# A four-layer modulated convolution and a mixture of experts on one core: layer 3 run one group later, routing two, tap matrices placed by the host, the first inputs scaled first

## The reference

```python
# x: (128 samples, 32 channels, 512 positions); four convolution layers, K = 3,
# whose weights are modulated per sample by a style and then normalised
s = style @ mw.T + mb
weight = SCALE * w * s[:, None, :, None]
demod = lax.rsqrt(jnp.sum(weight * weight, axis=(2, 3)) + EPS)
# layer 0 'same'; layer 1 'upsample' (transposed, stride 2, then blur);
# layer 2 'same'; layer 3 'downsample' (blur, then stride 2)
# its result, read as 4096 tokens of 512, goes through 16 experts, the best 4 for each token
scores = jax.nn.sigmoid(x @ gate_w.T) + bias
topk_w, topk_idx = jax.lax.top_k(scores, TOPK)
z = jax.nn.silu(x @ Wg.T) * (x @ Wu.T)            # for each expert, 256 wide
out = sum_over_chosen(weight * (z @ Wd.T)) + shared_expert(x)
return x_input + out
```

## Time and profile before

| | |
|---|---|
| three runs | 1251.31, 1252.97 (median), 1257.61 us |
| profiled execution | 1261.94 us, span 1260.2 us |
| PE busy, share of the span | 91% |
| DVE / ACT / POOL busy | 63% / 39% / 46% |
| mean clock granted to PE | 0.969 of full speed |
| first phase, to the last `place` | 569 us |

### The profile page before, as it was taken

How to read it: one execution, slowest core, us unless ns; L and a number is a source line. 1 busy time by engine, 2 the same in 40 slices (tenths; PEclk the granted TensorE clock), 3 DMA queues, 4 the chain that set the end, 5 groups by cost and what they waited for, 6 DMA issues and landing times. The chain is left out here.

```text
span 1260.2 us, 24634 instructions
## 1 busy us (share of the span) xinstructions
PE 1147.9 (91%) x7160; PEld 1001.8 (79%) x7161; DVE 799.0 (63%) x1979; ACT 497.6 (39%) x1164; POOL 577.8 (46%) x667
## 2 busy tenths in 40 slices
PE   3799998989898988772999999999999999999995
PEld 2577777777777766662999999999998889999995
DVE  6667776767776767655665565655656665555653
ACT  4555555555554545330332232323324332222321
POOL 1001423232323233344566656666566566666663
PEclk9999999999999999975999999999999999999998
DMA  4565444444444534314667676676766777666664
GB/s 147 134 178 140 135 133 134 134 130 137 132 135 117 146 108 132 90 34 118 150 119 157 115 157 118 124 150 110 156 118 151 197 118 165 109 111 112 113 113 74
DMA packets 141625, 162.42 MB, mean 129 GB/s; under 512 B 33120, under 2 KB 98720, under 8 KB 140064
## 3 DMA queue, kind: packets, MB, share of 16 engines
q0 software_dynamic: 35696, 74.34, 33.1%
q1 hardware_dynamic: 104608, 87.78, 23.9%
q10 hardware_dynamic: 1296, 0.01, 0.1%
HBM read 73.41 MB, written 55.18 MB: 102 GB/s over the span
## 5 line engine op out<-in xcount | busy, mean ns | idle before, releaser
L1262 PE MATMUL bank<-xt_hi,wup_hi 128*128 128x256 f32 x1104 | 276.2, 283 | 1.7 <-ACT xt_hi L635 1.6
L1262 PE MATMUL bank<-xt_hi,wup_lo 128*128 128x256 f32 x1104 | 275.7, 282 | 0.0
L462 POOL DMA_INDIRECT out_rows<-yb,sid x140 | 227.4, 1625 | 91.2 <-DVE yb L1029 67.1
L1262 PEld LDWEIGHTS bank<-xt_hi,wup_hi 128*128 128x128 f32 x1104 | 209.9, 190 | 6.6 <-ACT xt_hi L635 2.0
L404 POOL DMA_INDIRECT lists<-entry,place x128 | 130.8, 1022 | 177.8 <-DVE place L854 100.9
L1262 PEld LDWEIGHTS bank<-xt_hi,wup_lo 128*128 128x128 f32 x1104 | 209.3, 190 | 2.7
L545 ACT ACTIVATE t<-bank,cB,cA 128x256 f32<-128x256 f32 (+1 forms) x384 | 172.2, 539 | 68.7 <-PE bank L217 66.4
L449 POOL DMA_INDIRECT xg<-h_rows,gid x140 | 142.2, 1015 | 122.5 <-PE bank L1240 80.8
L1266 PE MATMUL bank<-xt_lo,wup_hi 128*128 128x256 f32 x1104 | 176.5, 282 | 0.0
L1266 PEld LDWEIGHTS bank<-xt_lo,wup_hi 128*128 128x128 f32 x1104 | 151.4, 190 | 0.0
L1029 DVE TENSOR_SCALAR yb<-bank,all_lists 128x512 f32<-128x512 f32 x138 | 99.6, 748 | 79.9 <-DMA out_rows<-yb,sid 46.0
(11 more groups left out here) (212 smaller groups left out, 2169.5 us busy)
## 6 DMA issues: line engine op xcount, KB each, us to landing
x<-x1p SPq DMA_DIRECT2D x64, 384.0 KB
wraw<-in_Wup SPq DMA_DIRECT2D x11, 1024.0 KB
xraw<-in_xq SPq DMA_DIRECT2D x32, 260.0 KB
xbase<-in_x SPq DMA_DIRECT2D x32, 256.0 KB
h_rows<-hrow SPq DMA_DIRECT2D x128, 64.0 KB
out_rows<-orow SPq DMA_DIRECT2D x32, 256.0 KB
x<-x1p SPq DMA_DIRECT2D x64, 127.0 KB
wdraw<-in_Wdn SPq DMA_DIRECT2D x11, 512.0 KB
```

The source lines that it names most:

```text
L462: pool.indirect_dma_start(out=out, out_offset=bass.IndirectOffsetOnAxis(ap=sid[:, u:u + 1], axis=0), in_=yb[:, u, :], in_offset=None, comp ...
L1262: pe.matmul(dst, lhs[a], rhs[0], start=k == 0 and a == 0, stop=False)
```

## The change

Three things. The tap matrices come placed (and the sum of squares is taken on 32 partitions), so that only the blur's mix and the split remain on the chip; POOL scales two groups before it does anything else, and DVE's constants for the routing move behind the scales. The pipeline becomes deeper: body g runs layer 3 of group g - 1 and the stage of group g - 2, each one body later, and G + 3 bodies are run in place of G + 2. The banks are dealt out anew (layers 1 and 2 share banks 1 and 2, layer 3 has bank 3, the logits bank 4), and the steps within a body stand in another order on each engine.

```diff
+        MATRICES = ((placed, 0, FIRST, 2), (placed, 2, SAME, 2), (mixed, 0, UP, 1), (mixed, 1, DOWN, 3))
...
+        def bodies(eng, body, end):
+            for g in range(R + 1):
+                body(g, None, None)
+            with eng.Fori(0, ROUNDS - 1) as it:
+                for u in range(R):
+                    body(it * R + (R + 1 + u), it, u)
+            for g in range(LAST + 1, end):
+                body(g, None, None)
...
@@ SP
-            for q in range(Q):
-                sp.dma_start(wnat[C * q:C * q + C].rearrange("o l i k -> o l (i k)"),
             sp.dma_start(xraw[:, 0], xq[0]).then_inc(S["x_loaded0"], 16)
+            sp.dma_start(placed[:, PLACED_UP:PLACED_DOWN], placed_taps[:, PLACED_UP:PLACED_DOWN]).then_inc(S["placed_loaded1"], 16)
+            sp.dma_start(placed[:, PLACED_DOWN:], placed_taps[:, PLACED_DOWN:]).then_inc(S["placed_loaded2"], 16)
...
+            def body(g, it, u):
...
+                if within(g, 0, G - 3):
+                    sp.wait_ge(S["x0_hi"], g + 2)
...
+                if within(g, 3, G + 3):
+                    sp.wait_ge(S["o_ready"], g - 2)
...
+                if within(g, 1, G + 1):
+                    sp.wait_ge(S["h_ready"], g)
                      for q in range(Q):
+                        sp.dma_start(h_rows[bass.ds(P * (g - 1), P), q * (L // Q):(q + 1) * (L // Q)].rearrange("(b c) w -> c b w", b=NB),
...
+                if within(g, 0, G - 1):
+                    stack(g + 1)
@@ POOL
+            pool.wait_ge(S["s_ready"], 1)
+            for g in range(2):
+                scaled(g, g % 2, g // 2)
             pool.wait_ge(S["fill_written"], 16 * 2)
@@ DVE
+            for to, m, at, weights, sem_name in ((0, 1, PLACED_UP, UPK, "placed_loaded1"), (1, 3, PLACED_DOWN, BK, "placed_loaded2")):
+                dve.wait_ge(S[sem_name], 16)
+                for n, weight in enumerate(weights):
+                    term = placed[:, at + n * m:at + n * m + m].rearrange("p t m -> p (t m)")
+                    mix = mixed[:, to:to + m].rearrange("p t m -> p (t m)")
...
+                many, number = settled(g, it, u)
+                if many:
+                    settle(number, 2 if many == R else (number - ROUNDS - 1) % 2, many)
                 if stage:
+                    dve.wait_ge(S["sg_ready"], g - 1)
...
+                if within(g, 0, G - 2):
+                    first_in(g + 2, odd)
                 for ph in range(2):
...
-                if tail < 1 and not (early and g == G - 2):
-                    first_in(g + 2, par, None)
@@ PE
-            for dst, at, n in [m for m in MATRICES if m[0] is not None] + [(5, SQ, 4)]:
-                for t in range(n):
-                    r = pe.transpose(bank[dst][:, P * t:P * t + P], big[:, at + t].rearrange("p q c -> p (q c)"), ident[:])
...
+                if within(g, 0, G - 1):
                     layer0(g + 1)
+                many, number = settled(g, it, u)
                 if many:
                     pe.wait_ge(S["mask_ready"], number)
...
+                if conv:
...
+                        pe.wait_ge(S["t3_ready"], g * 2)
...
                 if stage:
+                    pe.wait_ge(S["h_ready"], g - 1)
+                    if not (early and g == 2):
+                        pe.wait_ge(S["o_ready"], g - 2)
+                    for c in range(HC):
+                        r = pe.transpose(bank[5][:, P * c:P * c + P], hrow[:, odd, c, :], ident[:])
+                    r.then_inc(S["xt_t"], 1)
+                if within(g, 1, G + 1):
+                    if not (early and g == 1):
+                        pe.wait_ge(S["h_ready"], g - 1)
+                    dst = bank[3][:].rearrange("p (b w) -> p b w", b=NB)
...
+                    pe.wait_ge(S["x3_ready"], g * 4 - 1)
+                    hi_passes(pe, dst, terms)
+                    pe.wait_ge(S["x3_ready"], g * 4)
+                    lo_passes(pe, dst, terms).then_inc(S["l3_done"], 1)
```

More of the change, by code:

```diff
@@ L248, in routed, with within, half, settled @@
                             one()
[L251 to L273, removed]
+        MATRICES = ((placed, 0, FIRST, 2), (placed, 2, SAME, 2), (mixed, 0, UP, 1), (mixed, 1, DOWN, 3))
+        def within(g, least, most):
+            return not isinstance(g, int) or least <= g < most
+        def half(g, it, u, back):
+            return (g - back) // 2 if isinstance(g, int) else it * (R // 2) + (R + 1 + u - back) // 2
         def scored(g, u):
             if isinstance(g, int):
-                return 1 if g > LAST else R if g >= R and g % R == 0 else 0
+                return 0 if g > G + 1 else 1 if g > LAST + 1 else R if g > R and g % R == 1 else 0
             return R if u == 0 else 0
+        def settled(g, it, u):
+            if isinstance(g, int):
+                last = g - LAST - 1
+                return (0, 0) if last < 1 else (R, ROUNDS) if last == 1 else (1, ROUNDS + last - 1)
+            return (R, it + 1) if u == 2 else (0, 0)
+        def bodies(eng, body, end):
[6 more added lines that the diff above has]
+                body(g, None, None)
         block = ctx.enter_context(nc.Block())
@@ new lines, in body @@
+                if within(g, 1, G + 1):
+                    act.wait_ge(S["l3_done"], g)
+                    if not (first and g < 3):
+                        act.wait_ge(S[f"h_written{1 - odd}"], half(g, it, u, 1) * (16 * Q))
+                        act.wait_ge(S["xt_t"], g - 2)
+                    land(act)
+                    evac(g - 1, range(NB), bank[3][:].rearrange("p (b w) -> p b w", b=NB), hrow[:, 1 - odd], 3, S["h_ready"])
+                if stage:
+                    act.wait_ge(S["up_done"], g - 1)
+                    if not (first and g == 2):
+                        act.wait_ge(S["z_ready"], g - 2)
+                    act.activation(sg[:, 0, :], bank[6][:, 0:I], ACT.Sigmoid).then_inc(S["sg_ready"], 1)
@@ L619, in _ @@
             act.wait_ge(S["scales_ready"], 2)
-            for g in range(R):
-                body(g, 0, g % 2, (g // 2, (g + 1) // 2))
-            with act.Fori(0, ROUNDS - 1) as it:
-                for u in range(R):
-                    body(it * R + (R + u), u, u % 2, (it * (R // 2) + (R + u) // 2, it * (R // 2) + (R + u + 1) // 2))
-            for g in range(LAST, G + 1):
-                body(g, 0, g % 2, (g // 2, (g + 1) // 2), tail=max(0, g - G + 2))
+            bodies(act, body, G + 2)
             for c in range(HC + IC):
@@ L763, in _ @@
             dve.tensor_scalar(cB[:, 0, :], d[:, 1, :], cbias[:, 0:1], None, ALU.mult).then_inc(S["scales_ready"], 1)
+            for n in range(2, 4):
+                matrix_lo(n)
             link(inverse(2))
@@ L1125, in body @@
                     ins.then_inc(S["prefix_done"], 1)
-                if stage:
-                    pe.wait_ge(S["h_ready"], g)
-                    if not (early and g == 1):
-                        pe.wait_ge(S["o_ready"], g - 1)
-                    for c in range(HC):
-                        r = pe.transpose(bank[5][:, P * c:P * c + P], hrow[:, 1 - par, c, :], ident[:])
-                    r.then_inc(S["xt_t"], 1)
-                if tail < 2:
+                if conv:
                     if early and g == 0:
```

440 lines of the change are left out of this document (187 added, 253 removed).

## The result

The changed kernel takes 1270.05 us (median of four runs, 1266.98 to 1272.66) against 1255.29 (1251.31 to 1258.47) for the kernel before: 1.0112 times the time, 95% interval 1.009 to 1.0134. The forecast was 1230 with a range up to 1250.

The account below looks back on a forecast made before the run. PE, 91% busy, was taken as the bound, idle in loop waits. Start -8, five groups -3.4, loop -19.4, end +7 sum to -23.8: 1261.94 profiled becomes 1238, or 1229 from the median, stated as 1230; range 1219 to 1250.

Parts of the forecast that it names:

- the stack's landing: From the stack's first issue on SP to layer 1: 6.5 us taken, bounds 5.5 and 7.5.
- start: Up to layer 1 of group 0: x1p ready at 22 us instead of 30.05, -8 us.
- five groups: Layer 1 of group 0 to that of group 5: 71 us instead of 74.4, -3.4.
- loop: The 24 bodies in six turns: 366 us instead of 385.4, -19.4.
- end: Layer 1 of group 29 to the last place: 78.7 us instead of 71.6, +7, bounds +4 and +11.
- experts: The experts' phase behind the first phase: 691 us, not touched by the change.
- the sum's baseline: Whole kernel: profiled execution 1261.94 us, 9 above the median 1252.97; that excess was taken off the forecast too.
- waits for `x_lo` and `x2`: PE's loop waits for DVE's low part and `x2`, 0.47, 0.65 and 2.07 us, would go.
- wait for `mask`: PE would wait some 1.4 us before the prefix matmuls, once in a turn of the loop.
- Rival 3: Stack hidden in the loop: landing under 6.2 us, PE sets the pace, 1221 us; chance 0.14.
- Rival 2: Same pace as before: landing 7.2 to 7.8 us, loop gives 0 to 8, 1246 to 1256 us; chance 0.16.
- Rival 1: Stack sets a slower pace: crowded queues, landing 8 us or more, loop +14, some 1263 to 1268 us; chance 0.12.

Follow-up runs that it names:

- e1: Changed kernel with 32 unused bytes ahead of x1p and 224 behind x1, putting both back on multiples of 256 bytes; 1247.08 us, 0.9932.
- e2: Kernel before with x1p and x1 moved to 224 bytes past a multiple of 256; 1250.89 us, 0.996.
- e4: Kernel before with the change's start alone, pipeline and queues of before, x1p and x1 at 224 bytes past a multiple of 256; 1243.41 us, 0.9903.
- e15: Kernel before itself, unchanged, traced on the same chip as other experiments; one run, 1263.78 us.
- e7: Kernel before with the change's start alone, x1p and x1 on multiples of 256 bytes; 1256.64 us, 0.9942.
- e17: Kernel of e6 with POOL's four scatters of each group set apart by later waits; 1246.76 us, 0.9933.
- e3: Changed kernel with SP's stack of the next group issued ahead of the wait for hrow and of h_rows, tiles left at 224; 1244.74 us, 0.9905.
- e13: Kernel of e6 with ACT's loop written for two bodies run twelve times, not four bodies six times; 1256.01 us, 0.9934.
- e14: Kernel of e6 again, beside e13 on the same chip; 1259.2 us, 0.9958.
- e9: Changed kernel itself, run again on a chip with ACT's halts; 1285.49 us, 1.018.
- e6: Changed kernel with aligned x1p and x1, stack ahead of h_rows, prefix matmuls behind layer 3, orow ahead of choose and mark; 1251.19 us, 0.9927.

## Why the prediction was wrong

**The step that failed** is the stack's landing: "I take 6.5, the only row in which someone waits for it", with 7.5 as the upper bound. Where PE waited for it, it was 7.2 to 8.1 us, 7.6 in the middle. The row was right for its tiles, but the change moved the tiles, and I carried the duration over as if a DMA's time were a matter of its bytes and its queue alone. I looked for crowding (the bound from above), not for addresses; yet the diff's list of tables, which I costed at nothing, was what decided.

Put back where they were, the tiles make the forecast's sum come out within 4 us in each term. e1 against the working: start 29.1 (forecast 29.7), five groups 75.1 (71), loop 363.9 (366), end 81.2 (78.7), experts 690.7 (691). That is a span of 1240.0 for a forecast of 1236 (1238 less the 1.7 around the span). The five groups missed by 4: groups 1 and 2 wait 1.9 and 6.3 us for their stack even there. In the loop two errors offset each other: the body behind `mark` takes 16.0 and not 16.6, and the one beside the scatters 15.1 to 15.6 and not 14.7. That is luck.

**The second step** is the sum's baseline. Even e1 is only 8.6 us under the kernel before by medians (1255.69 less 1247.08), not 24; by the profiled executions it is 20 (1261.94 less 1241.99). I took the 9 us by which the profiled execution lay over the median as common to both kernels and subtracted them from the forecast. They weren't: e1's profiled execution lies 5 us below its median. The earlier trace rows end a stretch of 71.6 us that takes 62.8 in e2 and 61.5 in e4, whose order of work there is the same; in the profiled execution the turn waited 4.28 and 2.52 us for `hrow` behind ACT's halts of 4.75 and 2.99. e15's expectation of 62 could not be tested, since that chip halts: its stretch is 67. So the end's +7 is +19 against an undisturbed kernel before: a good absolute value set against a bad reference.

**What held.** The start gives 7.1 us (forecast 8) and lasts when alone (e7). The waits for `x_lo` and `x2` went, the loop's clock rose from 0.98 to 0.99. The wait for `mask` came, 0.9 and not 1.4 us in the loop. PE sets the pace at 14.5 to 14.7 us in the bodies of e17 that wait for nothing else (14.6 from layer 1 at 113.2 to 127.8), with the stack early and no halts. Rival 3, the stack hidden, is e3's loop: 366.7, no better than e1's, as the waits for `mask` and `orow` and some for the stack remain.

**The rivals.** Rival 2 had the loop right: at 7.2 to 7.8 us it gives 0 to 8, and it gave 2.3; it has no term for the five groups. Rival 1's outcome, a slower kernel, came true, but not by its mechanism: the landing stayed under its 7.9 in most bodies, scatters were not the main cause, and the loop is no slower; the five groups (+7.3) and the end (+11) did it. Its own terms (1253 - 8 + 14 + 4 + 8) give 1271, not the 1263 to 1268 that it states. I had given the five groups -3.4 without asking what the upper bound of the landing does there, where PE waits 22.7 us for the stack: 10.7 us over the forecast, the largest single miss after the loop's.

**What stays open.** Why ACT halts on some chips. It isn't the length of its loop (e13). In e14's trace 52 of 54.5 us of halts in the loop fall into runs of POOL's scatters (with pauses under 2.5 us counted in), which fill a third of the time; in e15 11 of 13, in e9 18 of 20. That is a coincidence in time and not a cause shown; e17 was to separate them and met a chip without halts. The queues that load instructions moved the same 24 packets in e14 as in e1, so no extra code loading is seen either. e6's own order never ran on a chip without halts; e17, with its scatters moved, comes nearest. And what the chip's halts and the fall of PE's clock each cost the change was not separated.

## What to carry to other kernels

A change that adds or drops tables moves every tile allocated behind them. Before a DMA's duration is carried over, compare where its tiles begin, modulo 256 bytes, in both kernels; 32 bytes of padding ahead of them were worth 23 us here. Ahead of subtracting a profiled execution's excess over the median, find the stretch in which it lies, and check the forecast's absolute time against it. And try a reordering on more than one chip: the same early stack was 0.9905 with one set of tiles on one chip, and 1.0045 and 1.0044 with better tiles on two others.

## What the runs showed of the hardware

- Four DMAs of 1022 KB in all, from SBUF to SBUF in rows of 512 bytes: 259 to 261 GB/s, issue 2.9 us and landing 6.45 to 6.5 in the first stack with tiles on multiples of 256 bytes; 222 to 230 GB/s, 3.4 us and 7.6 to 7.75 at 32 or 224 past one. In the loop of e1 6.3 to 6.5, and 6.9 to 7.6 in the body in which POOL scatters ahead of the stack and beside it.
- A DVE cast or copy of 0.16 us beside POOL's multiplication of 1.05 to 1.13 us ends with it (0.80 and 0.48 us); a DVE reduction of 0.57 us beside it keeps its length.
- The same body takes 17.2 us at a granted clock of 1.00 and 18.7 at 0.91 (the kernel before, bodies from 319.6 and 255.2).
- In the loop ACT stands still for 1 to 6 us at a time in twelve traces on three chips, and in none of six on two others; 5 to 69 us in all, by the order of work.
